# Tokens stage of an attention and ternary-matmul kernel: PSUM evacuations put off, integer chunks split in two, the input tile loaded in halves

## The reference, cut to what matters

```python
xn = _layernorm(x, axis=-1)                    # x: 1 x 8192 x 4096, float32
# attention: 16 heads, head size 256 (32 x 8 blades)
q, k, v = proj(Wq, bq), proj(Wk, bk), proj(Wv, bv)      # xn @ W.T + b
logits = einsum(q * rev * met, k) * scale + einsum(q * rev, wk(bias_weight), k)
attn_out = softmax(logits) @ v
# ternary matmul with quantized activations
s_w = mean(abs(w)); w_t = clip(round(w / (s_w + 1e-8)), -1, 1)
s_x = maximum(max(abs(xn), axis=-1) / 127, 1e-8)
x_q = clip(round(xn / s_x), -127, 127) * s_x
out = x + attn_out + x_q @ (w_t * s_w).T
```

## Time and profile before

| What | us |
|---|---|
| Median of 2 runs (6537.42 to 6542.11) | 6539.77 |
| The profiled execution, its own time | 6538.74 |
| Span of its slowest core (core 2) | 6536.9 |
| Spans of the other cores | 6510.5 to 6533.0 |
| First and last start of xn, the tokens stage | 597.9 and 3208.5 |
| TensorE busy, whole span | 4275.9 (65%) |
| VectorE busy | 2908.2 (44%) |
| ScalarE busy | 2786.1 (43%) |
| GpSimd busy | 1256.9 (19%) |
| Mean granted TensorE clock of core 2 | 0.835 |

### The profile page before, as it was taken

One profiled execution on the slowest core, in us unless ns is written; L12 is line 12 of the kernel. 1 busy time (PEld: TensorE's weight loads), 2 busy tenths in 40 slices (PEclk: granted clock), 3 DMA queues, 4 the chain that ended last, 5 costly groups with the idle time before them and its releaser, 6 DMA issues.

```text
span 6536.9 us, 83535 instructions; the slowest of 8 cores (6510.5 to 6536.9 us)
## 1 busy us (share of the span) xinstructions
PE 4275.9 (65%) x29052; PEld 2755.1 (42%) x29422; DVE 2908.2 (44%) x3031; ACT 2786.1 (43%) x3804; POOL 1256.9 (19%) x548
## 2 busy tenths in 40 slices
PE   1003666666666666666546888887887887887887
PEld 1002444444444444444414565554444444444444
DVE  4635888888888888888630000000112111112112
ACT  0023444444444444444435666665333333333333
POOL 0041444444444444444400000000000000000000
PEclk7555787777878888877778999998999999999999
DMA  5813222222222222222122000002111111111111
GB/s 207 307 52 122 87 88 87 86 76 78 86 88 87 87 87 88 87 87 87 62 108 83 11 8 11 8 11 84 51 43 68 59 43 67 60 43 60 65 45 49
DMA packets 148833, 492.02 MB, mean 75 GB/s; under 512 B 16586, under 2 KB 98507, under 8 KB 114894
## 3 DMA queue, kind: packets, MB, share of 16 engines
q1 hardware_dynamic: 148430, 486.65, 20.6%
HBM read 369.14 MB, written 117.44 MB: 74 GB/s over the span
## 4 chain that ended last, share of the span: by engine, by line
PE 54%; DVE 18%; issue 9%; ACT 6%; DMA 5%; POOL 4%; SPq 2%; DVEq 1%; ACTq 0%; another core or an unknown queue 0%; POOLq 0%; PEldq 0%; PEld 0%
PE pbf L950 15%; PE pbf L936 10%; PE pbf L700 7%; PE pbf L718 7%; PE pbt L914 7%; DVE cB L440 4%; POOL xst L429 4%; PE pbt L936 4%; DVE st_all L555 2%; DMA xst<-wf 2%; DVE xi2fm L907 2%; ACT xntok L625 2%; SPq L253 2%; PE pbt L662 1%; DMA q2sb<-q_scr 1%
## 5 line engine op out<-in xcount | busy, mean ns | idle before, releaser
L942 ACT ACTIVATE expS<-pbf,eb_exp 128x512 bf16<-128x512 f32 x1536 | 1054.6, 687 | 1543.3 <-PE pbf L936 1543.2
L950 PE MATMUL pbf<-Vres,expS 128*128 128x257 bf16 x8192 | 1245.6, 276 | 57.9 <-ACT expS L942 7.5
L936 PE MATMUL pbf<-q2sb,Kres 128*128 128x512 bf16 x2880 | 902.1, 393 | 422.4 <-DMA q2sb<-q_scr 413.2
L950 PEld LDWEIGHTS pbf<-Vres,expS 128*128 128x128 bf16 x8192 | 745.0, 98 | 753.8 <-issue 451.8
L429 POOL TENSOR_TENSOR xst<-xst,cC 128x1024 f32<-128x1024 f32 x272 | 598.4, 2230 | 1558.2 <-ACT cC L423 1558.2
L662 PE MATMUL pbt<-c_id,xntok 128*128 128x128 bf16 x2048 | 214.1, 285 | 998.7 <-ACT xntok L625 983.6
L451 POOL TENSOR_TENSOR xitok<-xitok,cB 128x1024 bf16<-128x1024 bf16 x256 | 624.9, 2451 | 400.5 <-DVE xitok L446 400.5
L662 PEld LDWEIGHTS pbt<-c_id,xntok 128*128 128x128 bf16 x2048 | 184.7, 130 | 1028.7 <-issue 1023.4
L907 DVE COPY xi2fm<-pbt 128x1024 bf16<-128x1024 bf16 x256 | 164.9, 686 | 1003.4 <-PE pbt L901 1003.4
L437 DVE TENSOR_SCALAR cF<-xst 128x1024 bf16<-128x1024 f32 x272 | 306.4, 1127 | 494.4 <-POOL xst L429 480.4
L971 DVE RECIPROCAL rec_sb<-pbf 128x1 f32<-128x1 f32 x128 | 21.1, 165 | 1121.2 <-PE pbf L950 1116.3
(11 more groups left out here) (104 smaller groups left out, 4188.0 us busy)
## 6 DMA issues: line engine op xcount, KB each, us to landing
xst<-x SPq DMA_DIRECT2D x64, 2048.0 KB, 7.9
xst<-wf SPq DMA_DIRECT2D x32, 2048.0 KB, 8.5
xi_scr<-xitok SPq DMA_DIRECT2D x64, 1024.0 KB, 5.3
xi2t<-xi_scr SPq DMA_DIRECT2D x64, 1024.0 KB, 5.1
xslb<-xsl SPq DMA_DIRECT2D x64, 256.0 KB, 6.1
out<-outsb SPq DMA_DIRECT2D x64, 256.0 KB, 2.0
xst<-wk SPq DMA_DIRECT2D x4, 2048.0 KB, 9.6
xst<-wv SPq DMA_DIRECT2D x4, 2048.0 KB, 8.9
```

Of the source, the lines that this page charges most:

```text
L936: op("tensor", lambda e, d=d, mc=mc, sb_=sbk[b], lt=lt: e.matmul(sb_, K_res[:, d, mc * 128:(mc + 1) * 128], q2_sb[lt % 2][:, d, :], start= ...
L942: op("scalar", lambda e, sb_=sbk[b], e3=i % 4: e.activation(out=expS[e3][:], in_=sb_, func=ACT.Exp, bias=eb_exp[:]), sem="ER")
L950: op("tensor", lambda e, lc=lc, e3=e3, mc=mc: e.matmul(pvs(lc, 0, 257), expS[e3][:, lc * 128:(lc + 1) * 128], V_res[:, mc, :], start=(mc = ...
```

## The change

Three things are done together, all in `p1`.

1. **Evacuations put off.** The transposes and projections stay where they are in TensorE's list. Their evacuations are collected as closures (`evq`, and the returned lists `qev`, `kev`, `vev`) and put later into ScalarE's list: q directly behind xn; transpose groups 0 and 1 between the S1 and S2 of chunks 0 and 1; k and groups 2 and 3 behind those chunks; v behind S2 of chunk 3.
2. **Rounding split in halves.** `em_cmps` becomes `em_cmps_a` (C and X1 of chunks 0 and 1, before tinies and makew) and `em_cmps_b` (chunks 2 and 3, behind makew). S1, S2 and E of chunks 2 and 3 now stand behind the smalls of the next tile; X2 and E alternate in pairs on GpSimd.
3. **Loads in halves.** A tile is read by two transfers of 2048 columns; the first waits only for the comparisons of chunks 0 and 1 of tile t-2, the second for those of chunks 2 and 3. `em_stats` waits for the second half after four of its eight `bn_stats`.

Six chunk operations of the tile before now stand between makew and the stats, and the stats have a second wait in their middle. The diff, cut to its core:

```diff
@@ em_load
+            sh = "LDH" if u % 2 == 0 else "LDHB"
+            if u >= 2:
+                wait("sync", "VT", 2 * (jb + 4 * (u - 2) + 2))
+            dma("sync", xst[u % 2][:, 0:2048],
+                d_x[u * 128:(u + 1) * 128, 0:2048], sem=sl)
             if u >= 2:
                 wait("sync", "VT", 2 * (jb + 4 * (u - 2) + 4))
-            dma("sync", xst[u % 2][:], d_x[u * 128:(u + 1) * 128, :], sem=sl)
+            dma("sync", xst[u % 2][:, 2048:4096],
+                d_x[u * 128:(u + 1) * 128, 2048:4096], sem=sh)
...
@@ the loop over t
-            em_cmps(t - 1)
+            em_cmps_a(t - 1)
             em_tinies(t)
             em_makew(t)
             vw_now = cnt["VW"]
...
+            ch_S1(js[0], p, 0, vw_now)
+            evq.pop(0)()
+            ch_S1(js[1], p, 1, vw_now)
+            ch_S2(js[0])
+            evq.pop(0)()
+            ch_S2(js[1])
+            for f in kev:
+                f()
+            evq.pop(0)()
+            evq.pop(0)()
             if t >= 1:
+                ch_X2(jp_[0], xi_tok[0][:, 0:1024])
+                ch_X2(jp_[1], xi_tok[0][:, 1024:2048])
+            ch_E(js[0], p, 0)
+            ch_E(js[1], p, 1)
+            em_cmps_b(t - 1)
             em_stats(t + 1)
             em_smalls(t + 1)
+            ch_S1(js[2], p, 2, vw_now)
+            ch_S1(js[3], p, 3, vw_now)
+            ch_S2(js[2])
+            ch_S2(js[3])
+            for f in vev:
+                f()
+            if t >= 1:
+                ch_X2(jp_[2], xi_tok[0][:, 2048:3072])
+                ch_X2(jp_[3], xi_tok[0][:, 3072:4096])
+            ch_E(js[2], p, 2)
+            ch_E(js[3], p, 3)
```

More of the change, by code:

```diff
@@ L544, in em_stats @@
             p = u % 2
-            sl = "LDX" if p == 0 else "LDXB"
-            wait("vector", sl, LDXc[u])
+            wait("vector", LDXc[u][0], LDXc[u][1])
             wait("vector", "VS", VS0 + 3 * u)
             wait("vector", "SSM", SSM0 + max(0, u - 1))
-            for i in range(8):
+            for i in range(4):
+                op("vector", lambda e, p=p, i=i: e.bn_stats(
+                    out=st_bn[:, i * 6:(i + 1) * 6],
+                    in_=xst[p][:, i * 512:(i + 1) * 512]), sem="VSF")
+            wait("vector", LDXc[u][2], LDXc[u][3])
+            for i in range(4, 8):
                 op("vector", lambda e, p=p, i=i: e.bn_stats(
@@ L635, in em_makew, with em_cmps_a @@
                 scalar2=st_bb[:, p:p + 1], op0=A.mult, op1=A.add), sem="VW")
-        def em_cmps(u):
+        def em_cmps_a(u):
             if not (0 <= u < NT):
@@ L645, in em_cmps, with em_cmps_b @@
             ch_X1(js[0], xi_tok[0][:, 0:1024])
+            ch_X1(js[1], xi_tok[0][:, 1024:2048])
+        def em_cmps_b(u):
+            if not (0 <= u < NT):
+                return
+            p = u % 2
+            js = [jb + 4 * u + q for q in range(4)]
             ch_C12(js[2], p, 2)
-            ch_X1(js[1], xi_tok[0][:, 1024:2048])
             ch_C12(js[3], p, 3)
@@ L650, in em_cmps @@
             ch_X1(js[3], xi_tok[0][:, 3072:4096])
+        evq = []
         def em_transp(u, g0, g1):
@@ L666, in em_transp, with ev, mk_evac, th @@
                         sem=("TPS" if jx == 7 else None))
[L667 to L671, removed]
+                def ev(g=g, gt=gt, bnk=bnk, half=u % 2, mp=m % 2, m=m):
+                    wait("scalar", "TPS", TPS0 + gt + 1)
+                    wait("scalar", "PRJ", max(0, m - 1))
+                    op("scalar", lambda e: e.copy(
+                        out=xn_fm2[mp][:, g * 8:(g + 1) * 8,
+                                       half * 128:half * 128 + 128],
+                        in_=pb_t[bnk][:]), sem="TEV")
+                evq.append(ev)
+        pev_cnt = {}
+        def mk_evac(semn, fn, pre=None):
+            if semn not in pev_cnt:
+                pev_cnt[semn] = cnt[semn]
+            pev_cnt[semn] += 1
+            val = pev_cnt[semn]
+            pbkv = pbk[0]
+            pev_hist.append((semn, val))
+            def th():
+                if pre:
+                    pre()
+                wait("scalar", "PBK", pbkv)
+                op("scalar", fn, sem=semn)
+                assert cnt[semn] == val, (semn, cnt[semn], val)
+            return th
         def em_proj_q(jm):
@@ L675, in em_proj_q @@
             wait("tensor", "TEV", TEV0 + 8 * (jm + 1))
-            wait("scalar", "KVQ", 160 * jm)
+            out = []
             for ch in range(4):
@@ L704, in em_proj_k @@
                 pbk[0] += 1
-                wait("scalar", "PBK", pbk[0])
-                op("scalar", lambda e, ch=ch, b=b: e.activation(
+                out.append(mk_evac("PEV", lambda e, ch=ch, b=b: e.activation(
                     out=k_sb[:, ch, :], in_=pb_f[b][:, 0:256], func=ACT.Identity,
-                    bias=bkT[:, ch:ch + 1]), sem="PEV")
-                pev_hist.append(("PEV", cnt["PEV"]))
+                    bias=bkT[:, ch:ch + 1])))
+            return out
         def em_proj_v(jm):
             jp = jm % 2
+            out = []
             for tc in range(2):
@@ L724, in em_proj_v @@
                 pbk[0] += 1
[L725 to L728, removed]
+                out.append(mk_evac("PEVK", lambda e, tc=tc, b=b: e.copy(
+                    out=v_sb[:, tc, :], in_=pb_f[b][:])))
             drain("tensor", sem="PRJ")
-            PEV_AT[jm] = (cnt["PEV"], cnt["PEVK"])
+            PEV_AT[jm] = (pev_cnt.get("PEV", cnt["PEV"]),
+                          pev_cnt.get("PEVK", cnt["PEVK"]))
+            return out
         def em_kvq_stores(mm):
@@ L788, in p1 @@
         dma("sync", d_xiscr[(NT - 1) * 128:NT * 128, :], xi_tok[0][:], sem="DMO")
-        em_proj_q(NMAC - 1)
-        em_proj_k(NMAC - 1)
-        em_proj_v(NMAC - 1)
+        for f in em_proj_q(NMAC - 1):
+            f()
+        for f in em_proj_k(NMAC - 1):
+            f()
+        for f in em_proj_v(NMAC - 1):
+            f()
         for mm in (NMAC - 2, NMAC - 1):
```

37 lines of the change are left out of this document (17 added, 20 removed).

## The result

The changed kernel takes 0.9404 of the time of the kernel before, 95% interval 0.9393 to 0.9415: 6% faster. Its profiled execution took 6151.21 us against 6538.74, 387.5 us less, where the prediction had 322 less (6217). The runs were on several chips, where the fastest execution of the kernel before took 6526 to 6537 us; a difference of some 10 us between two runs is therefore not told from none.

The account below looks back on a forecast made before the run. Bound: a chain through several engines, none full, at 41.74 us per tile. From xn at 624.6, 62 x 36.7 puts the last xn 309 earlier, 13 more behind it: 6538.74 - 322 = 6217, range 6150 to 6290.

Parts of the forecast that it names:

- case A: Chunks 2 and 3: X1 goes before E, the other X1 waits; stats start at 21.8, round closes at 35.8 us.
- the race of X1 and E: At chunks 2 and 3 both ask near 18.8; too close to call, so 36.7 us per tile was taken.
- B: Chunks 2 and 3: E goes first, both X1 wait for one E each; stats start 23.8, round closes 37.6 us.
- Two small terms: Stage ends: second tile's xn 4 us later, at 624.6; behind the last xn, makew and last X2 some 13 us earlier.
- Makew of odd tiles: Makew finds X2 of chunk 0 holding the shared ports and ends at 14.5, in odd tiles as in even ones.
- X1 and the lock: VectorE's X1 and GpSimd's operations exclude each other on shared ports, by the skill's rule; old rows could not show it.
- The stats beside GpSimd: VectorE's bn_stats do not suffer from GpSimd: 4.84 us without and 4.85 beside four E.
- The half-load: Second half issued at 18.9, lands in 5.2 us; bn_stats wait 0 to 0.3, taken as 0.2 us.
- v in front of xn: Rival: v evacuations delay xn past 0.6 us cover; at clock 0.89 6295 us, chance 0.04; at 0.81 6394, 0.02.
- All three signs: Forecast wrong if even rounds exceed odd by over 3 us, xn waits for v, or half-load wait passes 2 us.
- the lower level of TensorE's clock: Rival: TensorE at 1.2 GHz for projections, v ending at 72, about 7090 us; chance 0.04, shared with order working against itself.
- the pessimistic half-load: Rival: second half takes 7.8 us like a whole load, stats wait 2.5 per tile, 6372 us; chance 0.09.

Follow-up runs that it names:

- e10_s2_early: Changed kernel with S2 of chunk 0 moved ahead of group 0's evacuation and S1 of chunk 1 on ScalarE; 0.9588, 6259.1 us.
- e3_whole_load: Changed kernel with one whole load per tile behind the last comparison, so part 3 undone; 0.9876, 6476.9 us profiled.
- e11_evac_half_load: Kernel before with parts 1 and 3 (evacuations put off, loads in halves), rounding undivided; 0.9118, 5953.1 us.
- e4_v_behind_xn: Changed kernel with the v evacuations behind the next tile's xn instead of ahead of it; 0.9411, 6141.2 us at best.
- e5_xn_first: Changed kernel with the next tile's xn directly behind its smalls, ahead of S1 and S2 of chunks 2 and 3 and v; 0.9513, 6211.0 to 6219.0 us.

## Why the prediction was right, and where it missed

The direction came out, the mechanism in the even rounds (and in 11 of 31 odd ones), and there most of the chain to within a few tenths. For the even round above, counted from its bn_aggr's end at 1718.50, predicted and measured were: E of chunks 2 and 3 at 5.86 and 5.85; xn at 6.7 and 6.65; the first X2 from 10.08 and 10.01; makew's end 14.5 and 14.3; the first comparison's end 17.0 and 16.8, the fourth's 18.8 and 18.6; the stats' start 21.8 (case A) and 21.7; the close 35.8 and 35.5.

**The missed term is the race of X1 and E.** I took 36.7 per tile, the middle of A (35.8) and B (37.6). The trace shows A in even rounds: X1 starts at 1737.03 and E at 1737.08, 0.05 us later. No round of the stage has both X1 locked out, so B never came. So 35.58 instead of 36.7, 62 x 1.12 = 69 us. Two small terms nearly cancel: the second xn starts at 621.85 instead of 624.6, and behind the last xn 6.4 us are saved, not 13 (the spans of the slowest cores differ by 387.2, 380.8 of it up to the last xn). 6217 - 69 - 3 + 7 = 6152 against 6151 measured. The forecast for case A in all rounds was 6161; the measured time is 10 us below it, 1 us above the lower end of my own range. `e10_s2_early` shows that this place is worth about 100 us when E comes sooner; it does so by a second comparison that waits, not by a second X1.

**Makew of odd tiles, a step that failed.** I had makew end at 14.5 "for both kinds of tile". In the odd round above it ends at 16.35: xn is 8.6 us behind bn_aggr, so makew asks for the lock only when X2 of chunk 1 has it, and ends behind that. Comparisons and X1 then run free, the last comparison ends at 18.8 and the half-load is there at 24.35, both as forecast. That the round still takes 35.7 is luck in part. The stats' second four were due at 24.2 by case A, and the half-load at 24.1 to 24.5, so leaving case A gained nothing; the forecast held both numbers but did not foresee that the path would change.

**X1 and the lock.** The Trainium skill, "SBUF — State Buffer", section "SBUF: two separate sides", says that a VectorE operation with two SBUF inputs is locked out as well, by a GpSimd operation that reads SBUF. This trace agrees: line 446, never above 690 ns before, now has records up to 2616 ns.

**The stats beside GpSimd.** The 4.85 us that I called "beside four E" overlapped with them for only 2 us. The statement holds all the same: in the even round above the eight `bn_stats` (1740.17 to 1745.1) ran beside E and X2 throughout and took 2.46 and 2.47.

**The half-load.** 5.2 us by the row of equal size, 5.1 measured. I counted 0.2 us of wait; it was nothing in the even round read and 2.00 in the odd one, where it stands in place of the locked comparison and X1. Over the stage it is 37.7 us in 23 rounds. `e3_whole_load` shows that the halves are worth some 300 us to a kernel whose rounding is divided, and `e11_evac_half_load` that they are worth about nothing to one whose rounding is not.

**v in front of xn.** The cover of 0.6 us was gone, as that rival foresaw at a grant of 0.89: the k projection took 15.74 us in a window granted 0.90, and the second v evacuation waited 0.89 us. All three signs that I had named as refuting the forecast did occur: xn waits for v, starts of xn are 37.5 and 34.0 us apart, 3.5 different, and the half-load's wait passes 2 us (up to 2.34). Yet none of them cost time; `e4_v_behind_xn` takes all three away and keeps the pace. The signs were badly chosen: the length of a round is to be read from bn_aggr to bn_aggr, where the engine that closes it stands (35.5 and 35.7).

**The other rivals** (the lower level of TensorE's clock, the pessimistic half-load) did not occur; the granted clock of the stage rose from 0.80 to 0.84 in the window compared, where TensorE's busy time rose from 249.50 to 296.62.

**What the prediction did not ask** is whether all three parts help. The trace of the kernel before had the number. Counted on VectorE from bn_aggr to bn_aggr, the round of a pair that has no late S1 already ran at 32.2 us in the old order, below the 36.7 that I worked out for the new one:

```profile
1819.64 0.36 DVE L558 BATCH_NORM_AGGREGATE st_all<-st_all 128x2 f32<-128x48 f32 x1
1851.88 0.36 DVE L558 BATCH_NORM_AGGREGATE st_all<-st_all 128x2 f32<-128x48 f32 x1
```

Part 1 alone gives 5962, and v behind xn 20 us more. Parts 2 and 3 alone make the kernel slower; by the rows above that is the store held back by X2 behind a late E, with the lock at X1 and the half-load, though no run undoes one of these alone. In the full change part 2 costs 198 us. The rows show two places for it: xn stands behind two more S1 and S2, with VectorE idle for 6 to 8 us in a round, and the load has less work in front of it. `e5_xn_first` removes most of the idle time alone and gains nothing; that the two bind in turn is argued from that and from the rows, since no run removes both and keeps the rounding divided.

## What to carry to other kernels

Where an engine waits in list order for results that it only has to copy away, move the copies behind the work that others wait for; this one move was worth 9% here. Work out each part of a change by itself against the round that the engines would run without it: a part that looks like more overlap can put a wait in front of the engine that sets the pace. Before making an operation ready sooner, ask which operation of a neighbour it will then exclude.
